# Summing the two experts' rows of the last layer: by chunk, without GpSimd

## The reference

```python
ys = _geglu(xf @ Ws1 + bs1) @ Ws2 + bs2            # shared expert
logits = (xf @ Wr + br) / TAU                      # 12 experts
top_val, top_idx = jax.lax.top_k(logits, 2)
top_w = jax.nn.softmax(top_val, axis=-1)
yE = each expert's geglu layer, 128 -> 2 x 384 -> 128
yr = sum over the two chosen experts of top_w * yE
x = x + 0.5 * (ys + yr)
```

## Time and profile before

| what | us |
|---|---|
| median of three runs (lowest to highest) | 1368.52 (1367.81 to 1371.91) |
| the profiled execution | 1368.41 |
| its span, from first to last instruction | 1366.5 |
| busy: TensorE, VectorE, ScalarE, GpSimd | 1170.9, 927.8, 846.7, 793.0 |
| the stretch from the last scatter's issue to the end of the span | 23.9 |

### The profile page before, as it was taken

One profiled execution on the slowest core, in us unless ns is written; L12 is line 12 of the kernel. 1 busy time (PEld: TensorE's weight loads), 2 busy tenths in 40 slices (PEclk: granted clock), 3 DMA queues, 4 the chain that ended last, 5 costly groups with the idle time before them and its releaser, 6 DMA issues.

```text
span 1366.5 us, 36413 instructions
## 1 busy us (share of the span) xinstructions
PE 1170.9 (86%) x12703; PEld 876.3 (64%) x12704; DVE 927.8 (68%) x2479; ACT 846.7 (62%) x2476; POOL 793.0 (58%) x708
## 2 busy tenths in 40 slices
PE   5899898998979999789989899898788858768784
PEld 2666675776745555456768577685677835558783
DVE  6998669886956777698866888787432366653233
ACT  3999768998435545489985899954243524323442
POOL 6788348884653452288843887543566532166653
PEclk8999999999989999999999999999799989879997
DMA  7011100111000000000110001132355520145564
GB/s 221 18 25 25 28 16 9 31 27 27 18 1 3 3 3 3 2 9 21 25 35 10 19 21 25 25 89 66 107 164 175 175 72 0 31 117 173 162 189 117
DMA packets 69809, 78.21 MB, mean 57 GB/s; under 512 B 25095, under 2 KB 50502, under 8 KB 69510
## 3 DMA queue, kind: packets, MB, share of 16 engines
q1 hardware_dynamic: 64133, 64.70, 17.2%
q0 software_dynamic: 5504, 11.28, 2.9%
HBM read 54.60 MB, written 8.78 MB: 46 GB/s over the span
## 4 chain that ended last, share of the span: by engine, by line
PE 33%; DVE 8%; ACT 5%; DMA 4%; issue 3%; POOL 1%; POOLq 1%; another core or an unknown queue 1%; SPq 1%; ACTq 0%; DVEq 0%
PE bank L1849 10%; PE bank L1863 4%; PE bank L916 3%; ACT pB L795 2%; DMA arena<-arena 2%; PE bank L637 1%; PE bank L928 1%; PE bank L600 1%; PE bank L545 1%; PE bank L559 1%; PE bank L551 1%; PE bank L612 1%; DVE mx L721 1%; DVE X L2157 1%; PE bank L1837 1%
## 5 line engine op out<-in xcount | busy, mean ns | idle before, releaser
L2107 DVE SCALAR_TENSOR_TENSOR act_b<-bank,vec,gl 128x128 f32<-128x128 f32 x258 | 75.0, 345 | 178.5 <-PE bank L1849 65.0
L864 POOL TENSOR_TENSOR rn<-ss,mhalf 128x16 f32<-128x16 f32 x64 | 187.8, 2934 | 6.7
L1930 ACT ACTIVATE gl<-bank,vec 128x128 f32<-128x128 f32 x258 | 76.2, 365 | 124.8 <-PE bank L1849 103.0
L1849 PE MATMUL bank<-arena 128*128 128x128 f32 x1032 | 141.2, 290 | 2.1 <-DVE act_b L2107 1.7
L1849 PEld LDWEIGHTS bank<-arena 128*128 128x128 f32 x1032 | 131.9, 204 | 8.9 <-issue 4.9
L2184 POOL DMA_INDIRECT arena<-u_rows,inv_u x86 | 84.7, 985 | 69.2 <-remote 30.5
L795 ACT ACTIVATE pA<-bank,nb,rn 128x128 f32<-128x128 f32 x256 | 113.6, 485 | 3.0 <-DVE nb L726 3.0
L795 ACT ACTIVATE pB<-bank,nb,rn 128x128 f32<-128x128 f32 x256 | 113.4, 477 | 1.7 <-DVE nb L726 1.7
L2190 POOL DMA_INDIRECT y_rows<-stg,inv_u x86 | 84.8, 986 | 43.0 <-ACT stg L1937 22.9
L850 POOL TENSOR_TENSOR arena<-arena 128x512 f32<-128x512 f32 x64 | 81.7, 1276 | 45.1 <-DVE nb L726 34.3
L857 POOL TENSOR_TENSOR arena<-arena 128x512 f32<-128x512 f32 x64 | 81.4, 1273 | 43.0 <-DVE arena L689 15.7
(11 more groups left out here) (335 smaller groups left out, 3135.7 us busy)
## 6 DMA issues: line engine op xcount, KB each, us to landing
arena<-in_L_ffn_We SPq DMA_DIRECT2D x86, 384.0 KB
arena<-arena SPq DMA_DIRECT2D x64, 128.0 KB, 2.3
arena<-in_L_ffn_We SPq DMA_DIRECT2D x3, 768.0 KB, 7.5
arena<-U SPq DMA_DIRECT2D x32, 64.0 KB
u_rows<-U SPq DMA_DIRECT2D x2, 1024.0 KB, 5.9
U<-y_rows SPq DMA_DIRECT2D x8, 256.0 KB, 4.4
uT<-y_rows SPq DMA_DIRECT2D x8, 256.0 KB, 4.8
arena<-U SPq DMA_DIRECT2D x32, 63.5 KB
```

The lines of the kernel that those rows point to most:

```text
L864: pool.tensor_tensor(rn[:, q % 4, :, :], ss[:, 1, :].rearrange("p (a h) -> p a h", a=2), mhalf[:, :].rearrange("p (a h) -> p a h", a=2), A ...
L1849: m = pe.matmul(bank[q % 2][:, j * P:(j + 1) * P], we1[q][:, half * HR + j * P:half * HR + (j + 1) * P], xT[:, q, :], start=True, stop=True)
```

## The change

For k0 = 1, all four chunks are treated alike. When a chunk's two loads have landed, VectorE adds the four tiles of U weighted (four operations), while ScalarE scales the four tiles of uT in place. VectorE then waits for ScalarE and for its own four operations and adds uT in one 128x512 operation. GpSimd has no work behind the scatters. Loads and stores go in the order 0, 1, 2, 3. `add_experts` for k0 = 0 is as it was.

```diff
-        BY_POOL = (2, 3)
-        LA_ADDS = 2 * NCH
-        BACK = ((0, 1, 2, 3), (0, 2, 1, 3))
+        BACK = ((0, 1, 2, 3), (0, 1, 2, 3))
 
         def sums(k0, c):
-            return 2 * (k0 * NT + c * CT)
+            return 2 * NT + c * (CT + 1) if k0 else 2 * c * CT
 
         def wait_added(eng, k0, c):
-            if k0 and c in BY_POOL:
-                eng.wait_ge(s.p_sum, LA_ADDS + 2 * BY_POOL.index(c) + 2)
-            else:
-                eng.wait_ge(s.x_sum, sums(k0, c) + 2 * CT)
+            eng.wait_ge(s.x_sum, sums(k0, c) + (CT + 1 if k0 else 2 * CT))
...
-        def scale_experts(act, k0, c):
...
+        def scale_second(act, c):
+            act.wait_ge((s.gat0, s.gat1, s.gat2, s.gat3)[c], 16 * 4)
+            for t in range(CT):
+                g = gathered(1, c)[:, t, :]
+                m = act.activation(g, g, ACT.Identity, scale=wc[:, 1, c * CT + t:c * CT + t + 1])
+            m.then_inc(s.x_scaled, 1)
...
-        def add_scaled(pool, k0, c):
...
+        def add_last(dve, c):
             xc = X[:, c * CT:(c + 1) * CT, :]
+            dve.wait_ge((s.gat0, s.gat1, s.gat2, s.gat3)[c], 16 * 4)
+            dve.wait_ge(s.s_tmp, NCH * 2)
+            for t in range(CT):
+                dve.scalar_tensor_tensor(xc[:, t, :], gathered(0, c)[:, t, :], wc[:, 0, c * CT + t:c * CT + t + 1],
+                                         xc[:, t, :], ALU.mult, ALU.add).then_inc(s.x_sum, 1)
+            dve.wait_ge(s.x_scaled, c + 1)
+            dve.wait_ge(s.x_sum, sums(1, c) + CT)
+            dve.tensor_tensor(xc, xc, gathered(1, c), ALU.add).then_inc(s.x_sum, 1)
...
         def fin_dve(dve):
-            for c in (0, 1):
-                add_experts(dve, 1, c)
-
-        def fin_pool(pool):
-            for c in BY_POOL:
-                add_scaled(pool, 1, c)
+            for c in range(NCH):
+                add_last(dve, c)
 
         def fin_sync(sp):
             per_seq = out.rearrange("b (t p) d -> p (b t) d", p=P)
-            for c in (0, 2, 1, 3):
+            for c in range(NCH):
                 wait_added(sp, 1, c)
...
-            for c in BY_POOL:
-                scale_experts(act, 1, c)
+            for c in range(NCH):
+                scale_second(act, c)
...
             mx_pool(pool, 1)
-            fin_pool(pool)
```

More of the change, by code:

```diff
@@ L2158, in add_experts @@
                                              ALU.mult, ALU.add).then_inc(s.x_sum, 1)
-        def scale_experts(act, k0, c):
[L2161 to L2166, removed]
-        def add_scaled(pool, k0, c):
-            pool.wait_ge(s.s_tmp, NCH * (k0 + 1))
-            xc = X[:, c * CT:(c + 1) * CT, :]
[L2171 to L2176, removed]
+        def scale_second(act, c):
[5 more added lines that the diff above has]
+        def add_last(dve, c):
+            xc = X[:, c * CT:(c + 1) * CT, :]
+            dve.wait_ge((s.gat0, s.gat1, s.gat2, s.gat3)[c], 16 * 4)
[6 more added lines that the diff above has]
+            dve.tensor_tensor(xc, xc, gathered(1, c), ALU.add).then_inc(s.x_sum, 1)
         def mx_pool(pool, k0):
```

## The result

The changed kernel takes 1361.67 us (median of 9 runs, 1359.99 to 1369.6); the kernel before, in nine runs that include the three of the table above, 1371.91 (1367.81 to 1373.01). The ratio is **0.9947, 95% interval 0.9931 to 0.9963**: faster by 0.53%, or 7.3 us. Forecast were 1362.0 us and a ratio of 0.9952. The profiled execution has a span of 1360.5 us (1360.0 forecast).

The account below looks back on a forecast made before the run. GpSimd's DRAIN, behind the last sums, was taken to end the span. 3.0 us from an earlier last store plus 3.5 from the DRAIN gave 6.5 saved: 1362.0 us against 1368.52; range 1360.8 to 1365.8.

Parts of the forecast that it names:

- the earlier last store: End of the program: the last store lands at 1359.55, so SP's DRAIN comes sooner; 3.0 us saved.
- (a): Program's end: without its four sums, GpSimd's DRAIN ends 7.1 us behind the last scatter, at 1350.7; 3.5 us saved.
- (b): Last sums: with GpSimd idle, VectorE's operations cost 0.344 us each, four in a row 1.13 to 1.14 us.
- (c): Last sums: VectorE gets one 128x512 sum per chunk, taken as 0.69 us, upper end 1.63.
- (d): Last sums: ScalarE scales four tiles per chunk in 1.27 us; handoff to a waiting engine taken as 0.05 us.
- (e): Loads and stores in order 0, 1, 2, 3: arrivals keep their positions, cost nothing; earlier second store 0.8 us at most.
- (f): Waits added: VectorE waits for ScalarE before each whole-chunk sum, with the next chunk's four operations queued behind it.
- A: Rival: GpSimd's DRAIN stays last at the program's end, so only the earlier store counts: 1365.4 us; chance 0.13.
- B: Rival: the DRAIN holds back the last scatter, moving all load arrivals by 7.1 us: 1369.0 us, slower; chance 0.06.
- C: Rival: the DRAIN's work holds VectorE's sums up; last sum at 1358.0, 0.8 us later, 1362.7 us; chance 0.08.
- D: Rival: the tail gains as forecast, but something ahead of it (run spread 4.1 us) hides part; chance 0.03.

Follow-up runs that it names:

- experiments 1 and 2: Changed kernel plus a GpSimd memset waiting for the last sum: ratio 0.9991; kernel before plus a GpSimd DRAIN between last scatter and first sum: 0.9973.
- experiment 1: Changed kernel plus one 128x1 memset on GpSimd that waits for the last sum: ratio 0.9991 to the kernel before.
- experiment 5: Changed kernel plus a GpSimd DRAIN, then four unused GpSimd operations from chunk 1's arrival: 128x512 sums 1320.88 us, or memsets 1315.59 us; before 1322.73.

## Why the prediction was right

The mechanism was right in both of its parts: 3.3 us measured for 3.0 from the earlier last store, 3.5 for 3.5 from the DRAIN. That the median meets the forecast within 0.3 us is partly luck. The forecast started from three runs with a median of 1368.52, and nine runs gave 1371.91; the saving forecast was 6.5 us, and measured were 6.8 by the two tails, 7.3 by the ratio and 10.2 by the medians.

**(a) The DRAIN.** The step that made the forecast "faster" and not "the same": 3.5 us measured for 3.5. It ends 7.1 us behind the last scatter, as the earlier trace rows had it, and experiments 1 and 2 show the cause from both sides: a tiny late operation brings it back, an early DRAIN takes it away from the old kernel. The prediction took 7.1 us as a price of its own; it is one of about 0.08 us per indirect DMA, and both phases just happened to have 86. Its reading of 0.01 us where no indirect DMA had come before is of the chain, which shows a part of that DRAIN; the whole of it ends 0.07 us behind the operation. The page on the boilerplate DRAIN (the Trainium skill, VectorE: DVE Perf Modes, section "The DRAIN you can't avoid") gives a constant of about 12 ns on all five engines. SP's 7 ns agrees with it. GpSimd's DRAIN at the program's end doesn't: it ended 7.1 us behind all of GpSimd's work where 86 indirect DMAs had been issued.

**(b) and (c) VectorE's durations.** 344 ns and 692 ns, as taken (0.344 and 0.69). Why they were longer before, GpSimd's reads, is shown by experiment 5.

**(d) ScalarE.** 1.28 us for four, handoff 0.03 us (1353.43 to 1353.46), where 1.27 and 0.05 were taken. The prediction's order of who decides held: ScalarE for chunks 0 and 1 (the waits on L2159), VectorE for 2 and 3.

**(e) The order of the loads.** Counted from the last scatter's issue the pairs came at 6.2, 8.7, 10.5 and 12.1 us, against 6.2, 9.1, 10.8 and 12.3 before. So no cost of the earlier store is to be seen, but the last pair came at 11.7 to 12.7 us over six executions with the changed sums, so one of some tenths isn't excluded. Up to 0.4 us of it would be hidden, as VectorE takes chunk 3 up that long behind its pair.

**(f) The added waits** cost the 0.17 us of idle time shown twice on L2171, on chunks that had slack. Behind chunks 2 and 3 VectorE's wait for its own four additions took 0.1 us (1357.04 to 1357.15), where 0.04 was taken.

The last sum came at 14.4 us for 14.6. What sets it is chunk 1's pair, as the chain of waits after shows:

```profile
1347.32 4.81 DMA uT<-y_rows
...
1352.15 1.28 ACT uT L2159 x4
```

From there VectorE works on without a wait for a load, 5.69 us to the last sum, where 5.57 had been forecast. The pair itself came 0.3 us sooner than forecast, which is within its spread: in the executions with the changed sums it lay between 8.3 and 9.6 us behind the last scatter's issue. The tail's 17.1 for 17.4 are these two differences and 0.1 us less behind the last sum.

Of the rivals, A falls with experiment 1. B falls with the timeline after: SP issues its first load 2.38 us after the last scatter's issue, exactly as before (1344.97 less 1342.59, in the trace of before), though a DRAIN stood behind it. C falls too: chunk 0's additions and its sum ran from 1349.6 to 1351.6, mostly under the DRAIN, at 344 and 692 ns. D isn't borne out: the ratio's 7.3 us (5.1 to 9.5 by its interval) are no less than the tail's 6.8, though in the one profiled execution the last scatter came 0.8 us later.

## What to carry to other kernels

Look behind the last busy instruction: the span ends with the last engine's DRAIN, and GpSimd's is long when it has issued indirect DMAs, so give GpSimd nothing to do late, or let it drain where it is idle. Don't give GpSimd operations that read SBUF beside VectorE operations with two SBUF inputs on a path that sets the end: in experiment 5, 5.4 us of GpSimd's sums took 4 us from VectorE. One engine that does all the work undisturbed was faster here than three that share it. And a forecast of the whole time is no better than its base: the savings could be read from the trace, the 1368.5 us they were taken from could not be relied on to 3 us.

## What the runs showed that had not been expected

GpSimd's DRAIN costs about 0.082 us for each indirect DMA since the last one: 4.05 us for 49, 7.0 for 85, 7.09 for 86, and 0.1 or less where none came since. It is paid once, also by a DRAIN of its own placed where GpSimd is idle. Behind indirect DMAs just issued, two short DRAINs lasted 1.3 and 1.4 us longer than that rate; waiting for the landing fits one of them, the other is open.

The same kernel before took 1322.73 us in one set of runs and 1369.7 in two others: 3.4%, six times the effect studied. The traces show where it lies: some 42 of the 47 us are in the two stretches of expert tiles. Here are the 43 scatters of the last one, in the changed kernel and in the kernel with memsets of experiment 5, which have the same code up to there:

```profile
L2185 POOL DMA_INDIRECT y_rows<-stg,inv_u x43: 966/987/999, 1223.8 to 1343.4; - x43
```

```profile
L2185 POOL DMA_INDIRECT y_rows<-stg,inv_u x43: 964/987/1002, 1197.7 to 1295.8; - x43
```

From the first to the last it is 119.6 us in the one and 98.1 in the other, and in the first mixture 119.2 and 98.5, with each scatter as long on GpSimd as ever. What slows that stretch stays open; the record names the same chip for all three sets of experiments. Only ratios inside a set could show the effect.
